# DTW alignment and FFN on one core: token lengths added to the distances on TensorE, one clamp-and-scale behind each transposition

## The reference, cut to what matters

```python
def _layernorm(x): m, v = mean(x), var(x); return (x - m) / sqrt(v + 1e-5)

def _pairwise_euclidean(a, b):            # a: 64 ctx rows, b: 512 token rows
    aa = jnp.sum(a * a, axis=-1)[:, None]
    bb = jnp.sum(b * b, axis=-1)[None, :]
    return jnp.sqrt(jnp.maximum(aa + bb - 2.0 * (a @ b.T), 0.0))

def _align_one(small, large):
    D = _pairwise_euclidean(small, large)
    R = _dtw_cost(D)                      # R = D + min(up, left, diagonal)
    i_idx, j_idx, valid = _backtrack(R, 64, 512)
    contrib = small[i_idx] * valid[:, None]
    return zeros(512, 256).at[j_idx].add(contrib)

x = x + vmap(_align_one)(ctx, _layernorm(x))
x = x + quantised_ffn(_layernorm(x))      # 256 -> 1024 -> 256
```

## Time and profile before

| | us |
|---|---|
| three runs | 177.49, 178.14, 178.94 |
| median | 178.14 |
| the profiled execution, its own time | 177.57 |
| span of its profile | 175.8 |
| mean granted clock of PE | 0.823 |
| busy: DVE, PE, ACT, POOL | 152.1, 113.3, 107.6, 38.8 |

### The profile page before, as it was taken

One profiled execution on the slowest core, in us unless ns is written; L12 is line 12 of the kernel. 1 busy time (PEld: TensorE's weight loads), 2 busy tenths in 40 slices (PEclk: granted clock), 3 DMA queues, 4 the chain that ended last, 5 costly groups with the idle time before them and its releaser, 6 DMA issues.

```text
span 175.8 us, 3392 instructions
## 1 busy us (share of the span) xinstructions
PE 113.3 (64%) x1065; PEld 78.3 (45%) x1065; DVE 152.1 (87%) x724; ACT 107.6 (61%) x203; POOL 38.8 (22%) x102
## 2 busy tenths in 40 slices
PE   6999880000045894000009779999999999999991
PEld 6898760000033681000003326665666666666680
DVE  4899999999999999999999389998899989896361
ACT  3698467899997010135050189877777786878720
POOL 7777764000000000000000000023041323222250
PEclk9999996555555559755555999999999999999998
DMA  5997008400019930020212421006373738192848
GB/s 143 355 348 234 6 4 326 184 0 0 2 52 334 347 107 0 0 76 0 75 62 85 63 37 22 4 0 63 56 72 53 64 61 89 31 105 28 109 48 191
DMA packets 19553, 16.86 MB, mean 96 GB/s; under 512 B 5712, under 2 KB 19152, under 8 KB 19408
## 3 DMA queue, kind: packets, MB, share of 16 engines
q1 hardware_dynamic: 14288, 12.69, 22.7%
q0 software_dynamic: 3808, 3.67, 17.8%
q10 hardware_dynamic: 1440, 0.30, 0.8%
HBM read 7.48 MB, written 9.18 MB: 95 GB/s over the span
## 4 chain that ended last, share of the span: by engine, by line
DVE 45%; PE 35%; DMA 7%; SPq 4%; issue 3%; ACT 3%; ACTq 0%; DVEq 0%
PE y L1389 14%; PE h L1370 9%; DVE Y L1151 6%; DVE R L925 6%; DMA X<-in_x_dram 5%; PE t L1370 5%; SPq L356 4%; DVE A L897 3%; DVE enter L1134 3%; DVE carry L915 3%; DVE bcarry L1133 3%; DVE M L916 3%; PE e L1329 3%; DVE Y L1148 2%; DVE Dm L886 2%
## 5 line engine op out<-in xcount | busy, mean ns | idle before, releaser
L531 POOL DMA_DIRECT2D out_dram<-E x14 | 17.0, 1217 | 125.6 <-DVE E L1120 125.6
L1389 PE MATMUL y<-w2T,XT 128*128 128x256 bf16 x240 | 35.8, 273 | 0.0
L1389 PEld LDWEIGHTS y<-w2T,XT 128*128 128x128 bf16 x240 | 23.3, 98 | 14.0 <-DVE XT L1064 0.3
L719 ACT ACTIVATE h_int<-h,b_s 128x512 int16<-128x512 f32 x37 | 25.3, 686 | 4.9 <-PE h L1370 4.3
L1410 PE MATMUL h<-w1T 128*128 128x512 bf16 x21 | 6.9, 487 | 24.8 <-DVE enter L1134 24.8
L1370 PE MATMUL h<-M,w1T 128*128 128x512 bf16 x74 | 21.9, 380 | 0.8 <-ACT M L712 0.7
L1309 PE MATMUL t<-ident_bf,w_raw 128*128 128x128 bf16 x32 | 4.6, 312 | 25.5 <-ACT w_raw L653 23.9
L1110 DVE TENSOR_SCALAR XT<-h_int 128x1024 bf16<-128x1024 int16 x28 | 12.1, 439 | 8.2 <-ACT h_int L719 8.2
L1410 PEld LDWEIGHTS h<-w1T 128*128 128x128 bf16 x21 | 2.3, 120 | 29.0 <-DVE enter L1134 25.6
L719 ACT ACTIVATE h_int<-t,b_s 128x512 int16<-128x512 f32 x19 | 13.0, 686 | 3.4 <-PE t L1370 3.2
L1309 PEld LDWEIGHTS t<-ident_bf,w_raw 128*128 128x128 bf16 x32 | 3.1, 148 | 27.1 <-issue 24.1
(11 more groups left out here) (236 smaller groups left out, 298.9 us busy)
## 6 DMA issues: line engine op xcount, KB each, us to landing
X<-in_x_dram SPq DMA_DIRECT2D x8, 512.0 KB, 8.4
out_dram<-E POOLq DMA_DIRECT2D x14, 256.0 KB, 4.5
w_raw<-in_L_ffn_w_dram SPq DMA_DIRECT2D x2, 1024.0 KB, 5.8
out_dram<-b_s SPq DMA_DIRECT2D x2, 1024.0 KB, 5.9
out_dram<-b_s SPq DMA_DIRECT2D x2, 768.0 KB, 9.4
S<-in_ctx_dram SPq DMA_DIRECT2D x1, 512.0 KB, 4.3
out_dram<-E SPq DMA_DIRECT2D x4, 128.0 KB, 3.2
path_dram<-A SPq DMA_DIRECT2D x3, 160.0 KB, 1.8
```

Source lines behind the costliest of these rows:

```text
L531: nc.gpsimd.dma_start(tiles_out[:, b:b + 2, quad_of(g, 2 * h), :], res[:, g % 2, 2 * h:2 * h + 2, :], accum_op=ALU.add).then_inc(out_store ...
L719: nc.scalar.activation(h_int[:, g % 2, n, :], hidden_banks[i % 3][:, :], ACT.Identity, bias=b1_s[:, n:n + 1], scale=1.0 / W_ONE).then_inc( ...
L1389: mm = nc.tensor.matmul(results(g, t, t + 1)[:, 0, :], hq[:, g % 2, n, t * P:t * P + P], w2T[:, n, :], start=(n == 0 and not bias), stop=( ...
```

## The change: what it does

- POOL writes the sums of squares into columns 0 to 7 and 32 to 39 of a 128x128 tile `row_sums`, zero elsewhere. spread_rows(k) gets a ninth product, full size, with `row_sums` stationary and the identity moving (L1263 of the new kernel): it turns the sums to rows. ACT takes the square root of lanes and rows in one operation of 128x144, `deviations`: columns 0 to 15 are std by lanes, columns 16 to 143 are std by rows.
- DVE inverts 8 rows (32 to 39, 8x128) in place, inverse_rows, and the lanes (128x16), inverse_lanes.
- PE, add_lengths(k): four float32 products a load with 40 stationary rows of 128 and 40 moving rows of 128, onto all 128 partitions of the bank that dots(k) left open (start=False). Rows 0 to 7 weigh std with aa + D, rows 32 to 39 weigh 1/std with -D * eps. token_lengths, token_gap, the additions on DVE and both clamps go.
- DVE: behind each transposition there is one operation max(., 0) * (1/std).
- ctx_lengths makes rows 0 to 7 now: four products with a stationary 128x8, all on the first group of partitions. POOL fills three more constant tiles first, with two selections.
- dots(3) goes by pairs of q: first q = 0, 1 for both halves h, then q = 2, 3 for h = 0, add_lengths, q = 2, 3 for h = 1, add_lengths. turns(3) is split, spread_rows(3) stands ahead of dots(2), and the masks on DVE stand ahead of the transposition of load 2.

```diff
+            nc.gpsimd.memset(len_of[:, :], 0.0).then_inc(rows_const, 1)
+            nc.gpsimd.memset(row_sums[:, :, :], 0.0).then_inc(rows_const, 1)
+            nc.gpsimd.memset(row_weights[:, :, :, :], 0.0).then_inc(rows_const, 1)
...
+            for e in range(2):
...
+                nc.gpsimd.affine_select(out=weights, in_=weights, compare_op=ALU.not_equal, fill=-D * EPS, base=-GAP_AT,
+                                        pattern=[[-1, 2], [-2, NQ], [0, TW]], channel_multiplier=1).then_inc(rows_const, 1)
...
-                nc.gpsimd.tensor_tensor(centred_sum[:, us], gap_square[:, us], half_sums[:, us],
+                nc.gpsimd.tensor_tensor(row_sums[:, k, 0:2 * GAP_AT].rearrange("p (a m) -> p a m", a=2)[:, :, 0:B],
+                                        gap_square[:, us].unsqueeze(1).to_broadcast([P, 2, B]),
+                                        half_sums[:, us].unsqueeze(1).to_broadcast([P, 2, B]),
...
-                nc.gpsimd.tensor_tensor(spread_parts[:, k, :, :], centred_sum[:, us].unsqueeze(2).to_broadcast([P, B, NQ]),
+                nc.gpsimd.tensor_tensor(spread_parts[:, k, :, :], row_sums[:, k, 0:B].unsqueeze(2).to_broadcast([P, B, NQ]),
...
-            def token_lengths(k):
-                pool.wait_ge(gaps_made, k + 1)
...
-                for e in range(2):
-                    nc.gpsimd.tensor_tensor(
-                        lengths[:, k % 2, e, :, :].rearrange("p (h c) i -> p h c i", h=2),
-                        aa[:, :, HR * e:HR * e + HR].unsqueeze(2).to_broadcast([P, 2, CL, HR]),
-                        length_gap[:, k, e, :].rearrange("p (h c) -> p h c", h=2).unsqueeze(3).to_broadcast([P, 2, CL, HR]),
-                        ALU.subtract).then_inc(lengths_made, 1)
...
+            def last_roots(hs):
+                k = LOADS - 1
+                act.wait_ge(prods_made, 2 * k + 2 * (hs + 1))
...
+                part = half_of_load(norms[:, k, :, :, :], hs).rearrange("p (e c) i -> p e c i", e=2)
+                nc.scalar.activation(dst, part, ACT.Sqrt).then_inc(rooted, 1)
...
-                nc.scalar.activation(std[:, k, :, :], spread_bank(k), ACT.Sqrt, bias=shifts[:, eps_at:eps_at + 1],
+                nc.scalar.activation(deviations[:, k, :], spread_bank(k), ACT.Sqrt, bias=shifts[:, eps_at:eps_at + 1],
...
-            def token_gap(k):
-
-                act.wait_ge(rstd_ready, k + 1)
-                nc.scalar.activation(length_gap[:, k, :, :], rstd[:, k, :, :], ACT.Square,
-                                     scale=math.sqrt(D * EPS)).then_inc(gaps_made, 1)
...
+            act.wait_ge(rows_const, 5)
...
+            for e in range(2):
+                rows = of_q[:, :, :, 0:HR] if e == 0 else of_q[:, :, :, I - 1:HR - 1:-1]
+                nc.scalar.activation(row_weights[0:B, e, :, :].rearrange("p h (q i) -> p q h i", q=NQ), rows, ACT.Copy,
+                                     scale=float(D)).then_inc(aa_copied, 1)
...
             spread(0)
+            copy_xT(1, 2)
+            copy_xT(1, 3)
...
+            v.wait_ge(rows_const, 1)
+            for h in range(2):
+                lanes = slice(I * h, I * h + I)
+                nc.vector.scalar_tensor_tensor(out=len_of[lanes, h:h + (B + 2) * (NQ - 1) + 1:B + 2], in0=ctx_len[lanes, :],
+                                               scalar=1.0, in1=ctx_mv[lanes, :, 1], op0=ALU.add,
+                                               op1=ALU.add).then_inc(ctx_len_ready, 1)
...
             def scaled(k):
-                v.wait_ge(prods_made, 3 * k + 1)
-                nc.vector.tensor_tensor(flat(norms[:, k, :, :, :]), flat(turned_back[:, k % 2, :, :, :]), scale_by(k),
-                                        ALU.mult).then_inc(prods_made, 1)
-
-            def lengthened(k):
-                v.wait_ge(prods_made, 3 * k + 2)
-                v.wait_ge(lengths_made, 2 * k + 2)
-                nc.vector.tensor_tensor(flat(norms[:, k, :, :, :]), flat(norms[:, k, :, :, :]), flat(lengths[:, k % 2, :, :, :]),
-                                        ALU.add).then_inc(prods_made, 1)
...
-                nc.vector.tensor_tensor(part, back, rstd[:, k, :, us].unsqueeze(3).to_broadcast([P, 2, CL, HR]),
-                                        ALU.mult).then_inc(prods_made, 1)
...
-                nc.vector.tensor_tensor(part, part, lengths[:, k % 2, :, us, :], ALU.add).then_inc(prods_made, 1)
-                v.wait_ge(prods_made, done + 3)
-                nc.vector.tensor_scalar(part, part, 0.0, None, ALU.max).then_inc(prods_made, 1)
...
+                nc.vector.scalar_tensor_tensor(out=half_of_load(norms[:, k, :, :, :], hs), in0=back, scalar=0.0,
+                                               in1=scale.unsqueeze(2).to_broadcast([P, UL, HR]), op0=ALU.max,
+                                               op1=ALU.mult).then_inc(prods_made, 1)
...
+            def inverse_rows(k):
 
                 v.wait_ge(std_ready, k + 1)
-                nc.vector.reciprocal(rstd[:, k, :, :], std[:, k, :, :]).then_inc(rstd_ready, 1)
...
+                rows = deviations[GAP_AT:ROWS, k, SW:SW + P]
...
+                lanes = deviations[:, k, 0:SW]
...
-            scales(0)
...
+            inverse_rows(0)
+            for j in range(B // 2):
+                moments(LOADS - 1, j)
...
-            lengthened(0)
-            scales(2)
+            inverse_rows(2)
...
-                pe.wait_ge(ctx_len_ready, 1)
+                pe.wait_ge(ctx_len_ready, 2)
                 for q in range(NQ):
-                    mm = nc.tensor.matmul(bank23[0][TW * q:TW * q + TW, :, :].rearrange("p a b -> p (a b)")[:, 0:P], ctx_len[:, q:q + 1].to_broadcast([P, TW]), ident[:, :],
+                    mm = nc.tensor.matmul(bank23[0][0:B, :, :].rearrange("p a b -> p (a b)")[:, P * q:P * q + P],
+                                          len_of[:, B * q:B * q + B], ident[:, :], start=True, stop=True)
...
+            def dots(k, hs=(0, 1), qs=range(NQ)):
...
+                pe.wait_ge(xT_copied, (UL // 2) * k + max(qs) + 1)
+                for h in hs:
...
                     for e in range(2):
                         at = P * (2 * e + h)
                         for kk in range(KH):
-                            for q in range(NQ):
+                            for q in qs:
                                 tokens = XT[:, k % 2, 2 * q + h, kk, :] if e == 0 else XT[:, k % 2, 2 * q + h, kk, P - 1::-1]
                                 mm = nc.tensor.matmul(flat[TW * q:TW * q + TW, at:at + P], ST[:, q, kk, h, HR * e:HR * e + HR],
-                                                      tokens, start=(kk == 0), stop=(kk == KH - 1))
+                                                      tokens, start=(at == first and kk == 0), stop=False)
...
+            def add_lengths(k, hs=(0, 1)):
...
+                pe.wait_ge(rows_ready, k + 1)
...
+                    for e in range(2):
+                        at = P * (2 * e + h)
+                        rows = deviations[0:ROWS, k, SW:SW + P] if e == 0 else deviations[0:ROWS, k, SW + P - 1:SW - 1:-1]
+                        mm = nc.tensor.matmul(flat[:, at:at + P], row_weights[:, e, h, :], rows, start=False,
+                                              stop=(e == 1 and h == hs[-1]))
...
-                mm.then_inc(spread_done, 1)
+                        nc.tensor.matmul(spread_bank(k)[TW * q:TW * q + TW, UL * e:UL * e + UL].rearrange("p (h a) -> p h a", h=2),
+                                         lane[:, e, :], parts, start=True, stop=True)
+                nc.tensor.matmul(spread_bank(k)[:, SW:SW + P], row_sums[:, k, :], ident[:, :], start=True,
+                                 stop=True).then_inc(spread_done, 1)
```

More of the change, by code:

```diff
@@ L34 @@
 UL = 2 * CL
+SW = 2 * UL
+GAP_AT = TW
+ROWS = GAP_AT + B
 NG = NU // 4
@@ L609, in _ @@
                 copy_xT(2, j)
-                if j % 2:
-                    token_gap(j // 2)
             spread(2)
-            for j in range(UL // 2):
-                copy_xT(3, j)
-                if j == 1:
-                    token_gap(2)
+            copy_xT(3, 0)
+            copy_xT(3, 1)
+            spread(3)
             roots(0)
-            spread(3)
-            token_gap(3)
+            copy_xT(3, 2)
+            copy_xT(3, 3)
             roots(1)
             roots(2)
-            for hs in range(2):
-                roots(LOADS - 1, hs)
+            last_roots(0)
+            last_roots(1)
             act.wait_ge(ctx_rest, 1)
@@ L939, in _ @@
             load_moments(2)
[L940 to L942 removed]
+            inverse_rows(0)
+            for j in range(B // 2):
+                moments(LOADS - 1, j)
+            inverse_rows(1)
+            for j in range(B // 2, B):
+                moments(LOADS - 1, j)
+            inverse_lanes(0)
             turned(0)
             scaled(0)
[L945 to L946 removed]
+            inverse_rows(2)
+            inverse_lanes(1)
             turned(1)
             scaled(1)
[L949 removed]
+            inverse_lanes(2)
```

(43 more changed lines are left out.)

114 lines of the change are left out of this document (49 added, 65 removed).

## The result

The changed kernel takes 180.35 us (median of 4 runs, 180.09 to 180.74) against 178.13 for the kernel before beside it: a ratio of 1.0124 with a 95% interval of 1.0079 to 1.0169. It is slower by 2.2 us; the forecast was 179.9, and the range (177.9 to 181.2) held the time. Both medians rest on four runs. In the 94 runs of the kernel before that were made beside the experiments its medians are 178.56 to 178.90, and against those the changed kernel's 180.35 is 1.45 to 1.8 us slower.

The account below looks back on a forecast made before the run. DVE bounds the distance stage now; PE, with almost 6 us of room, would take over: 25.61 + 0.65 + 0.87 + 3.49 + 1.56 + 0.87 - 1.60 = 31.45, plus 1.79 is 33.24 against 31.49; 178.14 + 1.75 = 179.9 us, range 177.9 to 181.2.

Parts of the forecast that it names:

- The bound: Distance stage ahead of the scans: PE sets the end, last product at 31.45; DVE alone would be ready at 31.05.
- PE's end: PE's last product ahead of the scans moves from 25.61 to 31.45 us.
- ctx_lengths: On PE, 8 records four abreast (2 slots) become 8 slots on one group of partitions: +0.65 us.
- Row products, add_lengths and changes of shape: On PE: four row products +0.87, 16 products of two slots +3.49, 12 more changes at 0.13 +1.56 us.
- The pairs: dots(3) by pairs of q, two abreast instead of four: +0.87 us with one block overlapped, bounds 0 and 1.74.
- rival 1: On PE, second blocks of pairs don't pass the first, or PE stands still again: 180.8 us, chance 0.20.
- The waits: PE's three stands before 25.61 (0.37, 0.98, 0.23) go, as PE is no longer ahead of its inputs: -1.60 us.
- the stall marked issue: PE's stand of 0.98 us from 17.56 to 18.54, 0.72 of it marked issue; forecast to go.
- The tail: From PE's end to the first rearrangement: transposition 0.44, fused operation 0.43, last roots 0.67 and gaps, sum 1.79 us.
- The time: Rearrangement starts at 33.24 against 31.49, and the kernel's end moves as much: 178.14 + 1.75 = 179.9 us.
- Rival 2: PE's new work is cheaper, changes of shape at 0.05 or pairs that cost nothing: 178.9 us, chance 0.24.
- Rival 3: DVE stays the bound, with 40-row products in one slot and free pairs: 177.7, 176.4 with cheap reciprocals; chance 0.14.

Follow-up runs that it names:

- the late place in the kernel before: Kernel before with the order numbers moved behind load 3, ahead of the masks; 178.2 us, ratio 0.9981.
- In the gap: Kernel before with the order numbers between the two halves of load 3's statistics, where DVE stands for the last DMA of tokens; 178.08 us, ratio 0.9956.

## Why the prediction was right

**The bound.** Forecast: PE becomes the bound, DVE's part is hidden. The chain, the waits of 2.27 and 0.73, the 0.02 us that taking the reciprocals away was worth, and the earlier starts with less work on PE (0.25, 0.41, 1.46 and 1.77 us) bear it out.

**PE's end.** Forecast 31.45, measured 32.01. By its steps:

- ctx_lengths was put at +0.65. The step itself grew by 0.61 (0.36 us to the next work before, 0.97 after), but the next work that can be compared, the first spread_rows, moved only from 12.11 to 12.22, and that stand was GpSimd's. What took it back lies ahead of this step: the first eight transpositions take 1.52 us to the next work before (from 6.56, records of 388 ns at the median) and 0.98 after (from 6.38, 272 ns). Why they ran faster isn't shown; their weight load waited 0.3 us for a DMA before. The prediction looked only behind 8 us. As a move of PE's end the term was 0.54 too large.
- Row products, add_lengths and changes of shape were put at 0.87 + 3.49 + 1.56 = 5.92. From the chain: four times 0.42, and 1.08, 1.08, 1.09, 0.64, 0.65: 6.22. Two slots a product, and a change of rows only is a change; both as taken.
- The pairs were put at +0.87, with full overlap of one block. dots(3) took 2.34 (27.32 to 29.66) and 1.00, together 3.34, where undivided it takes 2.02. So +1.32: the term was half too small, and it came out midway between full overlap and the strict order of rival 1 (1.74). The interleaved records from 28.66 to 29.01 show what overlapped: three steps of the eight.
- The waits were put at -1.60, and the stall marked issue did go. But the prediction counted as waits all that bare slots don't fill, and rows 3 mark only 0.16 and 0.72 as idle. With PE never standing, dots(0) to the next work takes 1.93 (2.11 before), dots(1) to the work behind spread_rows 1.99 (3.12 before), and half of an undivided dots(3) 1.01 (1.10 before, where the prediction has a wait of 0.23). Together 1.40 went: the rest was changes of shape, which stayed.

These make 31.45 - 0.54 + 0.30 + 0.45 + 0.20 = 31.86; 0.15 is not accounted for. That the end came within 0.6 us is in part luck: the first error has the other sign than the next three.

**The tail.** 1.79 forecast, 33.67 - 32.01 = 1.66 measured.

**The time.** +1.75 was forecast for the start, +2.18 came, and the medians differ by 2.2. The start of the scans carried over to the last computing instruction, as assumed. The weights were issued 6.35 us later (32.03 against 25.68), ACT took them up 3.04 later after a stand of 0.76, and the stretch behind the start grew by 0.20 at most for it. That start and medians agree so well is luck too. The profiled executions differ by 3.17, and the one of before is among its fastest, with the last tokens early; the forecast put the move on top of the median all the same.

**The rivals.** Rival 1's mechanism (strict order) held by half in the price, though records did pass, and its other half (the stall marked issue) didn't come back. Rival 2 needed cheaper changes of shape, and they were not. Rival 3 was mis-built, though its condition didn't arise. Its 31.05 for DVE alone was nearly right: in the run without the products the start is 32.21, and less DVE's waits for PE, 0.95 and 0.40, that is 30.86. The step that failed is "and then PE ends at 28.84", which takes slots off PE alone. With more slots gone than that PE ended at 30.54, because the reciprocals stand ahead of the statistics that GpSimd and PE wait for; without reciprocals it ended at 29.07. Its 176.4 for cheap reciprocals doesn't follow either: with PE's start at 30.6 the gain ends at 0.9, 177.3.

## What to carry to other kernels

An operation taken off the engine that bounds is worth only what its replacement on the same engine leaves: here 4.1 us of additions and clamps went and 3.8 us of reciprocals on 8 lanes came. The reciprocal's time went by the elements of a row and not by its lanes: 0.94 us for 8x128, 0.21 to 0.25 for 128x16, 0.15 for 8x1. Count the slots of the engine that takes the work up to the point where its result is needed, changes of shape included, before moving anything; "64% busy" said nothing about the first 32 us. And where the bounding engine waits for a DMA of varying lateness, independent work belongs in that wait.

## What the runs showed that was not expected

**How far products pass each other.** In dots(3) of the changed kernel the records of q = 2, 3 (bank y) and of q = 0, 1 (bank e) alternate two by two from 28.66 to 29.01, at the pitch of four abreast (12 records in 0.35 us). The first pair of the later block starts with six records of the earlier one still to come, and no sooner, in all five traces that have the pairs. In the earlier trace rows eleven records ran ahead of a single earlier one. What sets this reach isn't shown; its price is that most of the idle half of the array stayed idle. "TensorE: Matmul & The Clock Gate", Part 3, "The mechanism", of the Trainium skill has matrix products start strictly in program order, which the interleaved starts contradict. In the price the measured 1.32 us lies midway between that order (1.74) and full overlap (0.87).

**GpSimd slows operations on DVE.** The order numbers take 0.67 and 0.56 us beside token_lengths, and 0.20 to 0.26 without it, in the changed kernel and at the late place in the kernel before. In the gap, L796 started 0.07 us ahead of token_lengths and took 0.24, L797 beside it took 0.55. The same goes for the scaling of load 2, 0.69 and 1.13. The Trainium skill, "SBUF — State Buffer", "SBUF: two separate sides", has a port pair that DVE and GpSimd share and that one of them locks for a whole instruction; these numbers agree with that. By the page it holds for an operation of DVE with two inputs in SBUF or in a mode that uses two ports; whether the order numbers run in such a mode no trace here shows. The forecast's account of DVE left out these 0.8 us.

**When the last tokens land.** The slowest of the eight loads of tokens takes either 9.0 to 9.3 us from issue to landing or 10.3 to 10.4, in every trace one or the other. The view of the loads' line, of the kernel before and of the one with only load 3 by PE:

```profile
DMA to landing us min/median/max: 5.3/8.4/9.1
DMA to landing us min/median/max: 5.0/8.3/10.4
```

It is late in five of the seven traces of the kernel before and its variants, where DVE stands 0.75 to 1.43 us for it; in the two others it stands 0.17 and 0.35. It is early in all seven traces of the changed kernel and its variants. The kernel before spreads from 177.29 to 179.38 over 35 runs. The changed kernel spreads over 0.65 in four runs, over 0.15 in four runs without the reciprocals, and over 0.50 in ten without products and reciprocals. But its other variants spread over 0.99 to 2.08. That the landing is the cause of the spread of the kernel before is inferred: only one trace of it was taken, with the DMA early. Nor is a row reciprocal that fills the wait needed for a narrow spread, since the kernel without it has one. Why the changed kernel's tokens were early each time stays open.
